# Attention layer with a quantised MLP on one core: weight splits moved a head ahead, q remainder before normalisation, first rows by ScalarE, last head and last store rearranged

## The reference

```
xn   = (x - mean(x)) / sqrt(var(x) + eps)                  # x: 2 x 1024 x 256
q    = (xn @ Wq + bq).reshape(b, 16, 1024, 128)            # a plain reshape
k, v = heads of xn @ Wk + bk, xn @ Wv + bv
attn = softmax(q k^T / sqrt(128) + causal mask) v          # 32 (batch, head) pairs
gate, up = xt @ Wg^T, xt @ Wu^T                            # weights: 4-bit codes x block scales
ffn  = (gelu(gate) * up) @ Wd^T
out  = x + attn @ Wo + bo + ffn
```

## Time and profile before

| | us |
|---|---|
| three runs | 1262.61, 1260.76, 1258.79 |
| median | 1260.76 |
| profiled execution | 1260.4 |
| its span, first to last instruction | 1258.6 |
| mean granted clock of PE in it | 0.992 |

### The profile page before, as it was taken

One profiled execution on the slowest core, in us unless ns is written; L12 is line 12 of the kernel. 1 busy time (PEld: TensorE's weight loads), 2 busy tenths in 40 slices (PEclk: granted clock), 3 DMA queues, 4 the chain that ended last, 5 costly groups with the idle time before them and its releaser, 6 DMA issues.

```text
span 1258.6 us, 20567 instructions
## 1 busy us (share of the span) xinstructions
PE 1225.3 (97%) x7556; PEld 1084.6 (86%) x7556; DVE 876.2 (70%) x1695; ACT 741.1 (59%) x1534; POOL 742.7 (59%) x784
## 2 busy tenths in 40 slices
PE   8999999999999999999999999999999999999997
PEld 7788888888889999779999888899899779899886
DVE  8877777776766676656777666667677666676664
ACT  4544444444676667556676665576667566666653
POOL 6445545553676667347676742676767337677753
PEclk9999999999999999999999999999999999999999
DMA  6100000000000000110000011010000200000001
GB/s 151 46 7 14 13 14 11 23 1 9 13 13 14 27 14 13 51 30 27 13 14 14 25 36 47 14 46 14 26 14 13 64 1 22 18 14 14 14 5 34
DMA packets 57331, 29.87 MB, mean 24 GB/s; under 512 B 16272, under 2 KB 57232, under 8 KB 57232
## 3 DMA queue, kind: packets, MB, share of 16 engines
q1 hardware_dynamic: 56016, 27.62, 7.9%
q10 hardware_dynamic: 1216, 0.93, 0.2%
HBM read 26.44 MB, written 2.10 MB: 23 GB/s over the span
## 4 chain that ended last, share of the span: by engine, by line
PE 88%; DVE 7%; ACT 3%; POOL 1%; issue 1%; DMA 0%; ACTq 0%; POOLq 0%
PE ps L41 26%; PE ps L43 26%; PE ps L42 26%; PE ps L1117 9%; ACT probs L480 1%; DVE pt_lo L832 1%; DVE xn_rows L736 1%; DVE probs L921 1%; PE ps L985 1%; DVE wq_lo L805 1%; DVE q_all L814 1%; POOL probs L699 1%; ACT pt_hi L466 1%; DVE stats L721 0%; ACT wq_hi L386 0%
## 5 line engine op out<-in xcount | busy, mean ns | idle before, releaser
L699 POOL TENSOR_TENSOR probs<-probs,inv_sum 128x128 f32<-128x128 f32 (+7 forms) x256 | 294.9, 1152 | 20.0
L696 POOL TENSOR_TENSOR inv_sum<-row_sum,minus_one 128x1 f32<-128x1 f32 x256 | 141.1, 551 | 258.2 <-ACT probs L480 257.1
L480 ACT ACTIVATE probs<-probs,neg_max 128x128 f32<-128x128 f32 (+7 forms) x256 | 198.8, 777 | 109.6 <-DVE neg_max L921 107.1
L466 ACT ACTIVATE pt_hi<-ps 128x512 fp32r<-128x512 f32 (+3 forms) x384 | 173.7, 488 | 92.1 <-PE ps L1117 89.1
L832 DVE TENSOR_TENSOR pt_lo<-ps,pt_hi 128x512 fp32r<-128x512 f32 (+3 forms) x384 | 200.8, 551 | 16.9 <-ACT pt_hi L466 16.7
L921 DVE CUSTOM_DVE_ANT_0 probs<-ps,mask_row 128x128 f32<-128x128 f32 (+7 forms) x256 | 192.0, 750 | 14.7 <-PE ps L43 8.2
L1117 PE MATMUL ps<-ident,probs 128*128 128x128 f32 x1152 | 169.6, 275 | 5.2 <-DVE pt_lo L832 3.9
L682 POOL TENSOR_TENSOR hid_lo<-act_buf,hid_hi 128x512 fp32r<-128x512 f32 x64 | 82.9, 1295 | 140.7 <-ACT hid_hi L420 140.7
L1117 PEld LDWEIGHTS ps<-ident,probs 128*128 128x128 f32 x1152 | 134.9, 142 | 18.7 <-issue 8.9
L42 PE MATMUL ps<-pt_lo,v_hi 128*128 128x512 f32 (+3 forms) x386 | 133.8, 347 | 0.0
L43 PE MATMUL ps<-pt_hi,v_lo 128*128 128x512 f32 (+3 forms) x386 | 133.5, 346 | 0.0
(11 more groups left out here) (151 smaller groups left out, 3394.4 us busy)
## 6 DMA issues: line engine op xcount, KB each, us to landing
wq_in<-in_wq SPq DMA_DIRECT2D x63, 128.0 KB, 2.3
kv_in<-in_wk SPq DMA_DIRECT2D x16, 256.0 KB, 2.5
wo_in<-in_wo SPq DMA_DIRECT2D x32, 128.0 KB, 2.0
kv_in<-in_wv SPq DMA_DIRECT2D x32, 128.0 KB, 2.3
out<-acc SPq DMA_DIRECT2D x8, 256.0 KB, 2.4
acc<-in_x SPq DMA_DIRECT2D x2, 512.0 KB, 5.5
raw<-in_gate SPq DMA_DIRECT2D x16, 64.0 KB, 1.7
raw<-in_up SPq DMA_DIRECT2D x16, 64.0 KB, 2.1
```

What stands on the lines that cost most here:

```text
L466: nc.scalar.activation(pt_blocks(pt_hi, i, ch), T[at % 2][:, 0:blocks * P].rearrange("p (a b) -> p a b", b=P), ACT.Copy).then_inc(pt_hi_do ...
L480: nc.scalar.activation(row, row, ACT.Exp, bias=neg_max[:, s % 16:s % 16 + 1], scale=-1.0, accum_out=row_sum[:, s % 16:s % 16 + 1]).then_in ...
L696: nc.gpsimd.tensor_tensor(inv_sum[:, at], row_sum[:, at], minus_one[:], ALU.pow).then_inc(inv_done, 1)
L699: nc.gpsimd.tensor_tensor(row, row, inv_sum[:, at].to_broadcast([P, (tile_of(h, i) + 1) * P]), ALU.mult).then_inc(probs_done, 1)
```

## The change

- **Weights of a group.** Blocks 0 to 3 of groups 1 to 3 are split in the head before the switch (6, 14, 22), two in step 1 and two in step 3, by ACT and now POOL instead of DVE (`W_FIRST`, `w_first`). In the first stage blocks 2 and 3 are split before the first q step, and each step splits blocks 2u+4 and 2u+5.
- **q remainder.** At a switch POOL's `q_low(h + 1, 0)` stands in front of the normalisation of step 6. In head 30 the split of head 31's right half goes from step 6 to step 3, ahead of the left half (`q_count`).
- **First rows.** DVE makes rows 0 and 1 only; the others are made by ACT as x * rstd + shift, with shift = -mean * rstd by one small DVE instruction for each group of four. The places of statistics, integers, codes, rstd and transposes of the first stage are redistributed (tables `ROWS_AT` to `RSTDS_AT`, `X_AFTER_Q`); `make_rows(2)` goes to step k = 1 of the MLP.
- **Heads 0 and 31.** In head 0 K0 of head 1 changes places with V3 and goes to bank O. In head 31 steps 3 and 4 are no longer eager, and PV right stands ahead of the last transpose.
- **Last store.** The last output job goes to two banks, is added in two halves of 256 columns, and these are stored by SP and ACT, 128 KB each.

```diff
-        JOBS[0] = {0: {EARLY: "V0"}, 1: {EARLY: "K1"}, 4: {EARLY: "V1"}, 5: {EARLY: "V2"}, 6: {EARLY: "V3"}, 7: {EARLY: "K0"}}
+        JOBS[0] = {0: {EARLY: "V0"}, 1: {EARLY: "K1"}, 4: {EARLY: "V1"}, 5: {EARLY: "V2"}, 6: {EARLY: "K0"}, 7: {EARLY: "V3"}}
+        W_FIRST = {1: (0, 1), 3: (2, 3)}
-        X_AFTER_Q = {2: 1, 4: 2}
+        X_AFTER_Q = {2: 1, 6: 2}
+        ROWS_AT = {0: (4, 5), 1: (6, 7), 4: (8, 9), 5: (10, 11), 6: (12, 13), 7: (14, 15)}
+        STATS_AT, SHIFT_AT = {2: 2, 4: 3}, {0: 1, 3: 2, 5: 3}
+        INTS_AT = {0: (1, 0), 1: (1, 2), 5: (2, 0), 6: (2, 2)}
+        CODES_AT, CODE_ROWS_AT, RSTDS_AT = {0: 0, 2: 1, 7: 2}, {1: 0, 4: 1}, {2: 2, 4: 3}
+        q_count = lambda h, half: 2 * h + (half if h + 1 < NH else 1 - half) + 1
+        w_first = lambda h, i: [(h + 2) // GROUP * HEADS + n for n in W_FIRST.get(i, ())] if new_group(h + 1) else []
-        eager = lambda h, i: len(pv_at(h, i)) > 0 or i in (0, 3, 4) or len(q_steps(h, i)) > 1
+        eager = lambda h, i: len(pv_at(h, i)) > 0 or (i in (0, 3, 4) and h + 1 < NH) or len(q_steps(h, i)) > 1
...
         @block.scalar
+            def row(t):
+
+                g = t // 4
+                act.wait_ge(shift_done, g + 1)
+                wait(act, xt_done, KC * (g - 1))
+                nc.scalar.activation(xn_rows[:, g % 2, t % 4, :], rows_acc[:, t, :], ACT.Identity, bias=shift[:, t:t + 1],
+                                     scale=rstd[:, t:t + 1]).then_inc(rows_done, 1)
...
+            row(2)
+            row(3)
             xn_high(0)
+            wq_high(2)
+            wq_high(3)
...
-                if i < 2 and new_group(h):
-                    for n in (2 * i, 2 * i + 1):
-                        wq_high((h + 1) // GROUP * HEADS + n)
+                for n in w_first(h, i):
+                    wq_high(n)
...
-                if i == 6 and (new_group(h) or h + 2 == NH):
-                    q_split(h + 1, 0 if new_group(h) else 1)
+                if i == 6 and new_group(h):
+                    q_split(h + 1, 0)
+                if i == 3 and h + 2 == NH:
+                    q_split(h + 1, 1)
...
         @block.gpsimd
-                if k % 4 == 1 and 2 < j < NJ:
+                if k % 4 == 1 and j < NJ:
                     make_rows(j)
...
+                if i == 6 and new_group(h):
+                    q_low(h + 1, 0)
                 pool.wait_ge(exp_done, s + 1)
...
+                for n in w_first(h, i):
+                    wq_low(n)
+                if i == 3 and h + 2 == NH:
+                    q_low(h + 1, 1)
+                if i == 4 and not new_group(h) and h + 1 < NH:
                     q_low(h + 1, 0)
-                if i == 6 and h + 2 == NH:
-                    q_low(h + 1, 1)
...
         @block.vector
-                if i < 2 and new_group(h):
-                    for n in (2 * i, 2 * i + 1):
-                        wq_low((h + 1) // GROUP * HEADS + n)
...
+            for t in range(2):
+                dve.wait_ge(last_product_done, t + 1)
+                row = rows_acc[:, SEQ // P + t, :]
+                nc.vector.tensor_tensor(row, LAST_BANKS[t][:, 0:DM], row, ALU.add).then_inc(last_sum_done, 1)
...
         @block.tensor
             transposes(end - 2)
+            with_v(NH - 1, 1, "right")
             transposes(end - 1)
-            with_v(NH - 1, 1, "right")
```

More of the change, by code:

```diff
@@ L280, in attention, with store_last @@
         kv_cols = lambda name, first, width: d[name].rearrange("(c p) n -> p c n", p=P)[:, :, first:first + width]
+        def store_last(eng, t):
+            tile = SEQ // P + t
+            eng.wait_ge(last_sum_done, t + 1)
+            eng.dma_start(out.rearrange("(t p) k -> p t k", p=P)[:, tile, :], rows_acc[:, tile, :]).then_inc(out_stored, 16)
         @block.sync
@@ L377, in _ @@
             store(1)
[L378 removed]
+            store_last(sp, 0)
+            sp.wait_ge(out_stored, 16 * (NT // 2 + 1))
         @block.scalar
@@ L505, in _ @@
                     weights_high(W_AFTER_Q[u])
+                for t in ROWS_AT.get(u, ()):
+                    row(t)
                 if u == 6:
@@ L603, in q_low @@
                 rows = q_all[:, h % GROUP, half * 32:half * 32 + 32, :].rearrange("p r c -> p (r c)")
-                low(q_of(h, half)[1], rows, q_of(h, half)[0], q_hi_done, 2 * h + half + 1, q_lo_done)
+                low(q_of(h, half)[1], rows, q_of(h, half)[0], q_hi_done, q_count(h, half), q_lo_done)
             def rstds(g):
@@ L658, in _ @@
             rstds(1)
+            wq_low(2)
+            wq_low(3)
             for u in range(8):
-                for n in (2 * u + 2, 2 * u + 3):
+                for n in (2 * u + 4, 2 * u + 5):
                     if n < HEADS:
                         wq_low(n)
[L663 to L668, removed]
+                if u in CODES_AT:
+                    make_codes(CODES_AT[u])
+                if u in CODE_ROWS_AT:
+                    make_rows(CODE_ROWS_AT[u])
+                if u in RSTDS_AT:
+                    rstds(RSTDS_AT[u])
             for k in range(STEPS):
@@ L729, in variances, with shifts, first_rows @@
                                         ALU.add).then_inc(eps_done, 1)
-            def rows(g):
+            def shifts(g):
                 dve.wait_ge(rstd_done, g + 1)
-                wait(dve, xt_done, KC * (g - 1))
-                for t in range(4 * g, 4 * g + 4):
+                tiles = slice(4 * g, 4 * g + 4)
+                nc.vector.scalar_tensor_tensor(shift[:, tiles], mean_var[:, tiles, 0], -1.0, rstd[:, tiles], ALU.mult, ALU.mult
+                                               ).then_inc(shift_done, 1)
+            def first_rows():
+                for t in range(2):
                     nc.vector.scalar_tensor_tensor(
-                        xn_rows[:, g % 2, t % 4, :], rows_acc[:, t, :], mean_var[:, t, 0:1],
-                        rstd[:, t:t + 1].to_broadcast([P, DM]), ALU.subtract, ALU.mult).then_inc(rows_done, 1)
+                        xn_rows[:, 0, t, :], rows_acc[:, t, :], mean_var[:, t, 0:1], rstd[:, t:t + 1].to_broadcast([P, DM]),
+                        ALU.subtract, ALU.mult).then_inc(first_rows_done, 1)
             def xn_low(g):
@@ L841, in o_low @@
                                                    hi.bitcast(F32), ALU.add, ALU.subtract).then_inc(o_lo_done, 1)
-            def integers(j):
-                for part in range(4):
-                    integer(j, part)
             statistics(0, 4)
             variances(0)
-            rows(0)
+            shifts(0)
+            first_rows()
             statistics(4, 8)
@@ L853, in _ @@
             xn_low(0)
-            integers(0)
+            for part in range(4):
+                integer(0, part)
             dve.wait_ge(bq_in, 16)
@@ L857, in _ @@
                 q_evacuate(0, u)
[L858 to L877, removed]
+                if u in STATS_AT:
+                    g = STATS_AT[u]
+                    statistics(4 * g, 4 * g + 4)
+                    variances(g)
+                if u in X_AFTER_Q:
+                    xn_low(X_AFTER_Q[u])
+                if u in SHIFT_AT:
+                    shifts(SHIFT_AT[u])
+                if u in W_AFTER_Q:
+                    weights_low(W_AFTER_Q[u])
+                if u in INTS_AT:
+                    j, part = INTS_AT[u]
+                    integer(j, part)
+                    integer(j, part + 1)
             for k in range(STEPS):
```

49 lines of the change are left out of this document (31 added, 18 removed).

## The result

| | before | after |
|---|---|---|
| median, us | 1260.06 (6 runs, 1258.72 to 1262.61) | 1229.13 (6 runs, 1228.93 to 1229.57) |
| profiled execution, us | 1260.4 | 1229.01 |
| its span, us | 1258.6 | 1227.2 |
| PE busy, share of the span | 97% | 99% |
| mean granted clock | 0.992 | 1.000 |

The ratio is 0.9754, 95% interval 0.9742 to 0.9767. The forecast was 1231.0 us, with a range of 1226.5 to 1238.

What follows compares the result with a forecast made beforehand. TensorE, busy 97% of the span, bounds the kernel, so only its waits and low-clock stretches can be won. The terms sum to -29.5 us, taking the median of 1260.76 to 1231.0 us, range 1226.5 to 1238.

Steps and rivals of the forecast that it cites:

- main case: The forecast's own case for the whole kernel: 1229 to 1234 us, chance 0.58.
- Reading PE's waits as what can be won: Whole kernel: TensorE's waits come to some 30 us, and the change aims at most of them.
- q stage: First stage, q projection: TensorE's waits for weights and rows go once ScalarE makes most rows for full VectorE; -4.5 us.
- The clock: After five TensorE waits the clock halves for 3.3 us; keeping it up brings -4.8 us at the three group switches.
- (a): Rival: the clock falls again behind the waits left before block 2 and in the last head; 1234.3 us, chance 0.13.
- Block 2: MLP: w_rows moved behind hid_lo gives a new 1.6 us TensorE wait, the act_buf wait vanishes; +0.9 us.
- V0: Heads 6, 14, 22: this product waits for vw_lo behind the added weight splits; +3.0 us for three heads.
- Last head: Head 31: earlier q split, -4.5 us with the clock; new order, leaving a 1.3 us wait, -3.2 us.
- (b): Rival: GpSimd bounds the q stage, half of 4.7 us stays, heads 6, 14, 22 cost 5; 1235.4 us, chance 0.12.
- (c): Rival: no new wait, ScalarE runs ahead and V0's margin suffices; 1227.1 us, chance 0.09.
- (d): Rival, group switches: first weights don't help, the second q step waits for its bank, 6.2 us stay; 1237.2 us, chance 0.06.
- (e): Rival, group switches: slower than before, the moved q_low holds up GpSimd's normalisation; 1262 us or more, chance 0.02.

Runs made afterwards that it cites:

- experiment 1: Kernel after, with weight blocks 0 to 3 of a new group split in the new head itself again, low parts on VectorE: 1235.78 us.
- experiment 4: Kernel after, with all sixteen rows of x made by VectorE again, the order of weight splits kept as changed: 1233.88 us.
- experiment 2: Kernel after, with q_low of a new group's first head behind the normalisation of step 6 again: 1241.99 us.
- experiment 6: Kernel after, with w_rows of block 2 back at the end of the q stage: 1228.08 us.
- experiment 3: Kernel before, with only q_low of a new group's first head moved in front of the normalisation of step 6: 1245.95 us.
- experiment 7: Kernel after, with q_split and q_low of the last head's right half in step 6 of head 30 again: 1233.02 us.
- experiment 8: Kernel after, with exp made at once again in steps 0, 3 and 4 of the last head: 1230.47 us.
- experiment 9: Kernel after, with the last transposes in front of the right half of the product with V again: 1230.00 us.

## Why the prediction was right, and by how much it missed

The range held the time, and the result lies at the low edge of the main case, 1.9 us under the forecast. The terms of the sum add up to -29.55 us; by the profiled executions 31.4 were won, by the medians 30.9. By its steps:

- *Reading PE's waits as what can be won*: right. Undone one by one, the parts cost 6.65, 12.9, 4.75, 3.9, 1.35, 0.9 and 0.8 us, 31.2 in all; less the 1.05 of block 2, which is a loss of the change, 30.2 beside the 30.9 between the medians. The parts hardly overlap. That the two sums lie so close is partly luck, since each kernel draws its own stretches of low clock: experiment 1 had two of them behind its waits for weights where the kernel before had one, and experiment 4 had one in the q stage where the kernel before had none.
- *The clock*: right as a mechanism, but the stretches were miscounted. The prediction counts five stretches at the low clock and has all five in its sum: three behind q_lo (4.8), one behind the longest wait for wq_lo, the 2.76 us one of the last head (1.6), and one behind the wait for pt_lo, within the order of the last head. The trace of the kernel before has a sixth, behind the 1.86 us wait for wq_lo in head 15 (the lines under experiment 1). Rival (a) says of just these waits, "those of 1.85 to 1.89", that they did not drop the clock; one of the three did. This sixth stretch is the -3.65 beside -2.07 and -2.08 in the table: 1.6 us, most of the 1.9.
- *Block 2*: the wait was 1.1 us, not 1.6. POOL came earlier than laid out, hid_lo by 4.23 us where PE had won 4.0, and w_rows took 1.48, where the sum had 1.55 or more. PE came to the transposes 1.16 us later against the q stage's end, and by the fifth F product 0.87 of that was taken back, where 0.7 had been counted: +0.29 for +0.9.
- *q stage*: 0.5 us less than forecast. The step "VectorE is full and POOL stands behind it" was right (experiment 4). "Under 0.2 us each" for the shifts was wrong: the first took 0.68 in the kernel after, and in one kernel the second took 1.53. That a short instruction waits for a whole one of GpSimd's was not thought of, though the 4.70 us of the earlier trace rows hint at it; it was hidden in the kernel after.
- *V0*: margin, splits and copies added up as laid out, 0.9 us each. The waits themselves are 0.65.
- *Last head*: all in place, the wait for probs 0.8 instead of 1.3. Its order was the term called least certain, and missed by 0.1.
- *Last store*: 0.15 forecast, nothing measured; too small to be right or wrong.
- *Rivals*: (a) the clock falls behind the new waits: it fell behind none of them (1.1, 0.65 to 0.7, 0.8 us), in no kernel. But it spoke of waits of 1.6 and 1.3 us, and these came out shorter, so waits of that length were not tried. (b) POOL as the bound of the q stage: not seen. No wait for wq_lo is left, and POOL stands idle for 4.1 us before the codes at 37.85, waiting for VectorE. (c) No new waits: half true of block 2. (d) and (e) fell with experiments 1 and 2; POOL's 1.7 us of room for q_low were 1.7 us.

What stays open: why the same 1.86 us wait is followed by the low clock in one head and not in the next, where 0.6 us of the gain of experiment 6 come from, and what the order of the splits in the q stage is worth without the rows on ScalarE.

## What to carry to other kernels

Where one engine is busy for 97% of the span, list its waits, find for each what stands in front of the releasing instruction on its engine, and move that or the instruction; such parts can be counted one by one and summed. Work put in front of a chain needs a look at the margin of that chain: two splits of 0.7 us in front of vw_lo cost 0.9 us, and one step later the same two cost 0.2 us or less. A short VectorE instruction that others wait for belongs where no long GpSimd instruction can be running.

## What was new of the hardware

**The clock behind a wait.** In the kernel before and those of experiments 1 to 4, 7 and 8, PE has nine waits of 2.7 to 2.9 us: eight are followed by a stretch at 1.2 GHz of some 3.3 us, one is not (experiment 7 shows one of each). Of fifteen waits of 1.8 to 2.2 us, nine are and six are not. Of the ten waits of 1.1 us, one in each kernel that has w_rows of block 2 moved, none is. The low clock sets in between the restart itself (experiments 7 and 8) and 1.6 us after it (the third wait of experiment 2). So a wait of 1.9 us costs 2.1 or 3.6 us, and a single profile shows one draw: where a forecast hangs on it, both belong in the range. The spread of the runs fits: 3.9 us over the six runs of the kernel before, which has nine waits of 1.85 us or more, and 0.6 over the six of the kernel after, which has none behind its start.

**The start.** The same 112 filler products took PE to the first transposes between 9.10 and 10.65 us. Products per us in the stretch from 4 to 5 us, and from 6 to 7, in the profile of experiment 7 and in that of experiment 9:

```profile
4.00:5.00 1.00, 1.00 (x18) 1.00 (x16) 0.86 (x3) 0.08 (x1) 0.00 (x0) 1.00 0.81 232
...
6.00:7.00 1.00, 1.00 (x22) 1.00 (x20) 0.42 (x1) 0.18 (x1) 0.82 (x2) 1.00 0.99 311
```

```profile
4.00:5.00 1.00, 1.00 (x12) 1.00 (x11) 0.92 (x3) 0.08 (x1) 0.00 (x0) 1.00 0.93 252
...
6.00:7.00 1.00, 1.00 (x12) 1.00 (x11) 0.00 (x0) 0.35 (x2) 0.87 (x2) 1.00 1.04 320
```

PE goes from 12 to 22 products per us early in one run and after 7 us in the other, while the clock column says 1.00 throughout. A rate of about half is what the low clock would give, but no row shows the clock there; what the rows show is that at the very start of a run the rate tells something that the column doesn't. An early rise brings nothing by itself here, since rows and splits of the q stage set the time of the first F product (37.5 to 38.3 us in all eleven).
